# A graph layer with residual and layer norm: the last pair's instruction lists in another order, M's blocks in other shapes, and narrow products during the first load

## The reference

```python
z_l = h @ W_lang.T;  z_g = h @ W_grav.T;  v = h @ W_V.T          # per graph, h is 256x512
A_l = max(cos(z_l, z_l), 0) * not_eye
A_g = exp(-|z_g - z_g'|^2 / (2 sigma^2)) * not_eye
K   = w * rows_to_one(A_l * adj) + (1 - w) * rows_to_one(A_g * adj)
out = layernorm(h + (K @ v) @ W_O.T)
```

## Time and profile before

| | us |
|---|---|
| median of 3 runs (lowest to highest) | 654.11 (653.62 to 655.98) |
| the profiled execution | 655.62 |
| its span, first to last instruction | 653.9 |
| PE busy | 641.2 (98%) |
| DVE busy | 533.6 (82%) |
| ACT busy | 383.4 (59%) |
| POOL busy | 136.1 (21%) |

### The profile page before, as it was taken

The page is one execution under the profiler, slowest core; times in us unless marked ns, Lnnn a source line. Parts: engine busy times, 40 slices in busy tenths (PEclk is TensorE's granted clock), DMA queues, the critical chain, the costliest instruction groups (busy, mean ns, idle before and its releaser), DMA issues.

```text
span 653.9 us, 10726 instructions
## 1 busy us (share of the span) xinstructions
PE 641.2 (98%) x2858; PEld 530.1 (81%) x2858; DVE 533.6 (82%) x1430; ACT 383.4 (59%) x707; POOL 136.1 (21%) x288
## 2 busy tenths in 40 slices
PE   8999999999999999999999999999999999999995
PEld 7888888888888888888888888888888888887774
DVE  5774979798897978888797978979797988978785
ACT  5453545656665565657556565756656566555665
POOL 2711011211211121121212112121211112112022
PEclk9999999999999999999999999999999999999999
DMA  9311757484665749386575928566683847454542
GB/s 294 76 54 51 176 160 175 119 246 104 210 158 174 197 134 246 85 256 140 165 177 174 226 80 259 127 193 150 186 209 111 250 104 229 109 167 140 161 136 106
DMA packets 141509, 106.48 MB, mean 163 GB/s; under 512 B 40112, under 2 KB 115632, under 8 KB 141488
## 3 DMA queue, kind: packets, MB, share of 16 engines
q1 hardware_dynamic: 140768, 104.40, 57.5%
q0 software_dynamic: 288, 1.05, 0.5%
q10 hardware_dynamic: 432, 0.79, 0.3%
HBM read 65.80 MB, written 40.40 MB: 162 GB/s over the span
## 4 chain that ended last, share of the span: by engine, by line
PE 92%; DVE 3%; DMA 2%; SPq 1%; ACT 1%; issue 1%; DVEq 0%; ACTq 0%
PE bank L1397 58%; PE bank L1485 17%; PE bank L1490 14%; PE bank L1442 2%; DMA work<-k_spill 1%; DVE p_lo L1033 1%; SPq L439 1%; DMA x_spill<-xs 1%; DMA r_row<-r_spill 1%; DMA xs<-in_L_gnn_W_lang 1%; PE bank L1420 0%; DVE work L1091 0%; DVE work L1148 0%; PE bank L1423 0%; SPq L422 0%
## 5 line engine op out<-in xcount | busy, mean ns | idle before, releaser
L735 ACT ACTIVATE p_hi<-bank,m_scale 128x512 fp32r<-128x512 f32 x128 | 85.8, 683 | 54.5 <-PE bank L1490 53.5
L1033 DVE SCALAR_TENSOR_TENSOR p_lo<-bank,m_scale,p_hi 128x512 fp32r<-128x512 f32 x128 | 94.0, 747 | 18.6 <-ACT p_hi L735 18.6
L1490 PE MATMUL bank<-hT_lo,m_hi 128*128 128x512 f32 x384 | 107.8, 389 | 0.0
L1397 PE MATMUL bank<-wvo_hi,hT_hi 128*128 128x512 f32 x256 | 99.7, 389 | 0.0
L1397 PE MATMUL bank<-wvo_hi,hT_lo 128*128 128x512 f32 x256 | 99.6, 389 | 0.0
L1397 PE MATMUL bank<-wvo_lo,hT_hi 128*128 128x512 f32 x256 | 99.6, 389 | 0.0
L1397 PE MATMUL bank<-p_hi,hT_hi 128*128 128x512 f32 x256 | 99.6, 389 | 0.0
L1397 PE MATMUL bank<-p_lo,hT_hi 128*128 128x512 f32 x256 | 99.6, 389 | 0.0
L608 POOL TENSOR_TENSOR rnorm<-norm,minus_half 128x2 f32<-128x2 f32 x32 | 34.8, 1088 | 245.1 <-DVE norm L1061 245.1
L1490 PEld LDWEIGHTS bank<-hT_lo,m_hi 128*128 128x128 f32 x384 | 72.1, 188 | 15.0
L739 ACT CAST v_hi<-bank 128x512 fp32r<-128x512 f32 x60 | 32.4, 590 | 62.6 <-PE bank L1397 62.6
(11 more groups left out here) (163 smaller groups left out, 1253.6 us busy)
## 6 DMA issues: line engine op xcount, KB each, us to landing
x_blk<-in_x SPq DMA_DIRECT2D x128, 128.0 KB, 3.5
x_spill<-xs SPq DMA_DIRECT2D x30, 512.0 KB, 3.8
xq<-x_spill SPq DMA_DIRECT2D x120, 128.0 KB, 3.5
x_nat<-in_x SPq DMA_DIRECT2D x30, 512.0 KB, 4.5
out_y<-y SPq DMA_DIRECT2D x30, 512.0 KB, 4.1
k_spill<-work SPq DMA_DIRECT2D x30, 256.0 KB, 2.2
work<-k_spill SPq DMA_DIRECT2D x120, 64.0 KB, 2.3
r_row<-r_spill SPq DMA_DIRECT2D x32, 128.0 KB, 3.5
```

The lines of the kernel that those rows point to most:

```text
L735: nc.scalar.activation(p_hi[:, :, j, g, :], src[:].rearrange("p (b n) -> p b n", b=2), ACT.Copy, scale=m_scale[:, g, j:j + 1]).then_inc(pr ...
L1033: nc.vector.scalar_tensor_tensor(out=p_lo[:, :, j, g, :], in0=src[:].rearrange("p (b n) -> p b n", b=2), scalar=m_scale[:, g, j:j + 1], in ...
L1397: last = pe.matmul(dst, lhsT, rhs, start=(n == 0), stop=(n == len(steps) - 1))
L1490: last = pe.matmul(pbank(k)[:], md_hi[:, g, 0] if i == 0 else m_hi[:, g, i, c], lo[i], start=False, stop=(i == DT - 1))
```

## The change

1. **Zeros.** POOL clears 128 columns instead of 512 before PE may start, and PE runs 35 products of 128 columns instead of 6 of 512.
2. **M's blocks.** Before, rows 0 to 3 of M were made from the diagonal on, 512, 384, 256 and 128 columns wide. Now row 0 is 512 wide and rows 1, 2 and 3 are 256 wide each: blocks 1 and 3, 1 and 2, 2 and 3. The number of blocks is the same, and of the off-diagonal ones the same six pairs are made once and mirrored once; which of the two is mirrored differs. All three MIRRORs now wait for the high part of row 3, where before MIRROR i waited for row i - 1. MIRROR G1 stands right behind UPPER G3 in PE's list. ACT copies one piece more for each M (row 2's mirror is two blocks apart).
3. **The last pair's lists** on SP, ACT, DVE and PE stand in another order, and the order of two steps on POOL is swapped. The same instructions are issued, the DMAs too.

```diff
+        def made(i, j):
+            return (i, j) in ((0, 1), (0, 2), (0, 3), (1, 3), (2, 1), (3, 2))
+        def row_blocks(row, i):
+            if i == 0:
+                return row
+            if i == 1:
+                return row.rearrange("p (k two n) -> p k two n", two=2, n=P)[:, :, 1]
+            return row[:, (i - 1) * P:(i + 1) * P]
...
-        WARM = 6
+        WARM = 35
...
-            nc.gpsimd.memset(kt_hi[:, 0].bitcast(F32), 0.0).then_inc(warm_ready, 1)
+            nc.gpsimd.memset(kt_hi[:, 0, 0, 0].bitcast(F32), 0.0).then_inc(warm_ready, 1)
...
-                        last = pe.matmul(dst[:, cols], lhsT, rhs, start=(n == 0), stop=(n == len(steps) - 1))
+                        last = pe.matmul(row_blocks(dst[:], i), lhsT, rhs, start=(n == 0), stop=(n == len(steps) - 1))
                 elif kind == MIRROR:
 
-                    pe.wait_ge(prep_lo, prepared(UPPER, g, i - 1))
-                    for r in range(i):
+                    pe.wait_ge(prep_hi, prepared(UPPER, g, DT - 1))
+                    for r in [r for r in range(DT) if made(r, i)]:
...
-                pe.matmul(kv_bank[1][:], kt_hi[:, 0, 0, 0], in_kt(kt_hi, 0), start=True, stop=True)
+                pe.matmul(kv_bank[1][:, 0:P], kt_hi[:, 0, 0, 0], kt_hi[:, 0, 0, 0], start=True, stop=True)
...
-            last_gram_turn(p, 0, L)
             k_times_v(q, 0, 0)
             k_times_v(q, 0, 1)
-            last_gram_turn(p, 0, G)
```

More of the change, by code:

```diff
@@ L139, in diagonal_blocks, with mirrored_blocks @@
             return (flat[:, 0:(DT - 1) * step].rearrange("p (i w) -> p i w", w=step)[:, :, 0:P], flat[:, (DT - 1) * step:])
+        def made(i, j):
[6 more added lines that the diff above has]
+            return row[:, (i - 1) * P:(i + 1) * P]
+        def mirrored_blocks(tile, i):
+            row = tile.rearrange("p (k n) -> p k n", n=P)
+            if i == 1:
+                return row.rearrange("p (a two) n -> p a two n", two=2)[:, :, 0]
+            return row[:, 0:2] if i == 3 else None
         def split_blocks(tile, g):
@@ L512, in _ @@
             q = p - 1
+            spread_r(q, 1)
             return_x(q, 1)
-            spread_r(q, 1)
             spill_k(q, 0)
+            return_k(q, 0)
+            load_x(q, 0)
+            spill_k(q, 1)
+            store(q - 1, 0)
+            return_k(q, 1)
+            store_r(p, 0)
             load_last(0)
             load_x(q, 1)
[L518 to L524, removed]
             spread_r(p, 0)
             store_r(p, 1)
+            store(q - 1, 1)
+            spread_r(p, 1)
             load_last(1)
-            spread_r(p, 1)
             store(q, 0)
-            store_last(0, 1)
             store(q, 1)
             store_last(0, 0)
+            store_last(0, 1)
             store_last(1, 1)
@@ L666, in _ @@
                 layer_norm(q, b)
-            for b, t in ((0, 1), (0, 0), (1, 0), (1, 1)):
+            for b, t in ((0, 0), (0, 1), (1, 0), (1, 1)):
                 last_spread(b, t)
@@ L698, in prep_hi_part @@
                 if kind == MIRROR:
-                    nc.scalar.copy(m_hi[:, g, i, 0:i * P], src[:, 0:i * P]).then_inc(mirrored, 1)
+                    if i == 2:
+                        for j in (0, DT - 1):
+                            c = slice(j * P, (j + 1) * P)
+                            last = nc.scalar.copy(m_hi[:, g, i, c], src[:, c])
+                    else:
+                        last = nc.scalar.copy(mirrored_blocks(m_hi[:, g, i], i), mirrored_blocks(src[:], i))
+                    last.then_inc(mirrored, 1)
                     return
                 if kind == UPPER:
-                    nc.scalar.copy(m_hi[:, g, i, i * P:], src[:, i * P:]).then_inc(prep_hi, 1)
+                    nc.scalar.copy(row_blocks(m_hi[:, g, i], i), row_blocks(src[:], i)).then_inc(prep_hi, 1)
                 else:
@@ L878, in _ @@
             proj_hi_part(p, 5)
+            normalise(q - 1, 0)
             proj_hi_part(p, 6)
             proj_hi_part(p, 7)
+            squares(q - 1, 1)
             gauss_scaled(q, 1)
-            normalise(q - 1, 0)
-            normalise(q - 1, 1)
+            save_x(p, 0, 0)
             proj_hi_part(p, 8)
-            save_x(p, 0, 0)
             save_x(p, 0, 1)
+            centre(p, 0)
             kt_hi_part(q, 0)
@@ L889, in _ @@
             save_x(p, 1, 1)
+            last_gauss(0)
+            centre(p, 1)
+            normalise(q - 1, 1)
             kt_hi_part(q, 1)
-            centre(p, 0)
-            centre(p, 1)
-            last_gauss(0)
+            squares(q, 0)
+            proj_hi_part(p, 9)
             last_gauss(1)
-            squares(q, 0)
             last_gauss_scaled(0)
             normalise(q, 0)
-            proj_hi_part(p, 9)
+            squares(q, 1)
             proj_hi_part(p, 10)
@@ L1435, in prepare @@
                 elif kind == UPPER:
-                    cols = slice(i * P, D)
-                    steps = three_products(rows, w_parts[g], w_parts[g], cols)
+                    hi, lo = w_parts[g]
+                    steps = [s for k in range(DT)
+                             for s in ((hi[:, k, rows], row_blocks(hi[:, k], i)), (hi[:, k, rows], row_blocks(lo[:, k], i)),
+                                       (lo[:, k, rows], row_blocks(hi[:, k], i)))]
                     for n, (lhsT, rhs) in enumerate(steps):
@@ L1614, in _ @@
             x_tile(p, 1, 1, 1)
+            last_gram_turn(p, 0, G)
             last_gram_turn(p, 0, L)
```

87 lines of the change are left out of this document (42 added, 45 removed).

## The result

The changed kernel takes 652.68 us (median of 17 runs, 652.14 to 653.80), the kernel before 654.43 in the same series (17 runs, 653.61 to 656.46): ratio 0.9969, 95% interval 0.9960 to 0.9978. It is faster by about 1.75 us, 0.3%, which is less than the 0.5% that the prediction took for a difference. It is 3.3 us above the 649.4 that was forecast, and outside the range of 647.0 to 652.2. The profiled execution took 652.80 with a span of 651.1, 2.8 less than that of before.

The account below looks back on a forecast made before the run. PE, busy 641.2 of 653.9 us, was taken as the bound. Terms -3.3 (last pair), -1.0 (end), -0.7 (M's blocks), -0.2 (zeros) sum to -5.2: 650.4 from the profile, 648.9 from the median, forecast 649.4, range 647.0 to 652.2.

Parts of the forecast that it names:

- The zeros: Start of PE's timeline: 35 narrow products at 0.17 us each instead of six wide ones, taken as -0.2 us.
- the middle case that I took: Start: clock up at 6.0, within the zeros, first block from 6.65 to 9.4, a gain of 0.65 us.
- That rival: Start: narrow products don't raise the clock, first block slow throughout, loss of 2.1 to 3.8 us; chance 0.08.
- The last pair: PE's waits in the last pair, for p_lo and centred xs, go by reordered lists: -3.3 us, from -1.5 to -3.9.
- The tail rival: Last pair: DVE's list or a landing sets the pace, half the gain gone, 651.3 us; chance 0.25.
- The end: Behind the last product: stores leave before any `store_last`, two 256 KB writes remain; -1.0 us, bounds 0 and -1.6.
- M's blocks: Products making M for L and G, new row widths, with a new wait before MIRROR G1: -0.7 us, bounds -1.1 and 0.
- The three good terms: The last pair at -3.3 us, the end at -1.0 and M's blocks at -0.7.

Follow-up runs that it names:

- the MIRROR edit: Changed kernel with eight wide products of zeros, and mirrored blocks waiting only for the highest row they turn instead of row 3: 649.05 us, ratio 0.9914.

## Why the prediction was wrong

**The zeros, the step that failed.** It had two parts, and both were off. "I take 0.17 as the nearest row": it is 0.215, the upper bound of the step, twice the 0.11 between two loads at 2.4 GHz. The 0.17 was the distance from the first product of a row of wide ones to the load behind it; it was no price of a load. That moves the block from 7.0 to 8.6. The larger part is "With the same 4.9 from 1.06 it is up at 6.0": I counted the narrow products like wide ones. Sixty of them left the clock at 1.2 GHz, and 35 of 256 columns in the same rhythm brought it up at 4.8, 3.6 behind the first. Behind narrow products the rise came only within the block: 2.3 (60), 3.5, 4.1 and 5.2 (35, three profiles) and 3.1 us (17) from its start, 3.8 with no zeros. The term was +3.0 in the profile and +4.1 by the medians, instead of -0.2, and the middle case that I took (rise in the row) is what no profile with this width shows. That rival stood in the prediction at 0.08, with 8.8 and 12 to 13.7 for the two times, which is what came; it had too little weight, as I had no row that showed a narrow product raising the clock and priced it as if I had. Its total of 651.5 to 653 holds the result. (Its own terms, a loss of 2.1 to 3.8 in place of the gain of 0.2, make it 651.7 to 653.4, which holds it too.)

For the price of a narrow product, the Trainium skill ("TensorE: Matmul & The Clock Gate", Back-to-back issue gap) has N / 1.2 GHz, 107 ns for 128 columns; by that the 35 would have ended at 4.8. But it gives this for a product by itself, and says in the same place that in a stream of weight loads and products both set the distance, so that the formula counts too little where the products are narrow. The trace agrees with that warning: 0.215 each, with a new load of fp32r weights for every product. The prediction used the formula without it.

**The last pair: -3.6, forecast -3.3.** Both waits went whole, and the run with SP's old list shows that they go by the other engines' order; SP asking for `r_row` earlier, which the prediction counted with it, was not needed. The new wait ahead of `last_k_times_v(1, 0)` was 0.26 where 0.3 was taken. The tail rival, which gave half back, shows nowhere: no wait of PE for `r_row` or a landing in the changed kernel.

**The end: -1.35, forecast -1.0**, within the bounds, and by the mechanism named: the store out of the last writes' way. Undoing that swap alone costs 1.3.

**M's blocks: -0.8, forecast -0.7**; the wait at MIRROR G1 is 0.55 where 0.6 was taken.

**From profile to median.** The three good terms make -5.75 in the profile. Against the profiled 655.62, with +3.0 for the zeros, that gives 652.9; 652.80 was measured. Without the zeros the medians show a little more than the -5.75: 648.39 against 654.40. The start is one reason why the 3.0 of the profiles is too little for the medians: behind six wide products and a gap of 0.5 the rise came at about 4.8 (the changed kernel with the old zeros), 6.9 (the blocks alone), 9.5 (the lists alone) and 9.8 (before), so that profile of before was a late one, and more can be lost against an early one. The zeros cost 2.6 in before and 4.1 in the new kernel; the intervals (1.6 to 3.4, 2.9 to 5.4) just overlap, so this difference may be noise. If it is none, whether a part of it comes from PE's waits in the last pair of before, which the new lists took away, lowering the clock in some of its runs was not tried and stays open.

## What to carry to other kernels

Products that are put in only to bring PE's clock up have to be tried in the width that is meant. Here 35 and 60 of 128 columns left it at 1.2 GHz, and 35 of 256 columns, which cost the same 0.21 us each, brought it up at 4.8. More of them than fit ahead of the data delay everything behind them. Price an operation by a row in which it is itself the limit, not by the distance that two rows happen to have; and where a forecast rests on a behaviour that no row shows, weigh the case without it at least equally. Orders on several queues are one design: the order of two stores on SP was worth 1.3 us at the end, and the other engines' lists with the wrong SP list took some 12 us longer than with theirs.

## What the runs showed of the hardware

- A narrow and a 256-column product on new fp32r weights cost the same 0.214 us at 1.2 GHz. In the five profiles with narrow zeros (17, three times 35, 60) the row has the same mean distance of 0.21 to the end; with 35 of 256 columns it fell to 0.12 within the row. Whether the load or the narrow product itself takes the 0.214 is not separated by these runs. The clock column of the windows doesn't show this start: it stands at 1.00 in the changed kernel while products cost 0.215, so the distance between products has to be read.

```profile
1.00:5.00 4.00, 3.92 (x19) 1.00 0.79 264
```

- DVE's `diagonals`, which read two tiles of SBUF, took 1.2 to 1.4 us instead of 0.28 while POOL ran tensor_tensor, and the low-part subtraction at 17.22, which reads one of its two inputs from a PSUM bank, kept its 0.68 beside POOL's at 17.29. The transfers are not the reason: in the kernel with 17 products of 256 columns the diagonal at 17.17, between two of POOL's operations, took 0.28 with the DMA share at 1.22 of its window, as high as beside the long ones (1.22 to 1.24). The Trainium skill ("SBUF — State Buffer", SBUF: two separate sides) has the port pair of DVE and GpSimd as an exclusive lock, held for the whole instruction, which a DVE operation with two SBUF inputs needs too; the trace agrees: about one POOL operation (2.59 / 2 = 1.3) is what the diagonal waited.
- The same overlap costs nothing when one diagonal falls into it, as in the changed kernel (1.38 at 18.62), and 2.2 to 4.3 us up to project 0 when several do. In three profiles a faster start moved the kernel into that case.
- PE's clock can fall after waits within the work as well, and not always does. With the old zeros it was at 1.2 GHz from 22 to 25, behind waits of 0.5 and 1.8 us at 18 to 20; with SP's old list likewise behind 0.4 and 1.95, and again behind the 6.5 us at 636. In the kernel with the MIRROR edit, behind 0.3 and 2.05 at the same place, it stayed at 2.4 GHz. The same window (busy and products, clock, DMA share, GB/s) with the old zeros and with the MIRROR edit:

```profile
22.00:23.00 1.00, 1.00 (x7) 0.50 0.00 0
```

```profile
22.00:23.00 1.00, 1.00 (x11) 1.00 0.00 0
```
